# First attention: the order in which GpSimd's subtraction walks its tile

## The reference, cut to what matters

```python
disp = (x @ W_disp).reshape(B, T, nh, bd).transpose(0, 2, 1, 3)
val = (x @ W_val).reshape(B, T, nh, hs).transpose(0, 2, 1, 3)
disp_win = _windows(disp, delta)          # the last 64 positions of each t
val_win = _windows(val, delta)
strain = disp_win - disp[:, :, :, None, :]
bond_act = gelu(strain @ W_strain + rel_emb @ W_pos)
bond_logits = (bond_act @ W_bond)[..., 0]
damage_act = gelu(strain @ W_dmg + b_dmg)
damage = sigmoid((damage_act @ W_dmg_out)[..., 0] + b_dmg_out[0])
logits = bond_logits - 10.0 * damage
weights = softmax(where(cmask, logits, -inf))
out = einsum('bntd,bntde->bnte', weights, val_win) ... @ W_cproj
```

## Time and profile before

| | us |
|---|---|
| runs before, median of 3 | 2930.57 (2927.01 to 2932.88) |
| profiled execution, from its first to its last instruction | 2936.9 |
| GpSimd busy in the whole span | 1076.2 |
| of it in the changed line, 128 instructions | 531.7 |
| ScalarE, VectorE, TensorE busy in the whole span | 1983.8, 2199.1, 2435.7 |

### The profile page before, as it was taken

One profiled execution on the slowest core, in us unless ns is written; L12 is line 12 of the kernel. 1 busy time (PEld: TensorE's weight loads), 2 busy tenths in 40 slices (PEclk: granted clock), 3 DMA queues, 4 the chain that ended last, 5 costly groups with the idle time before them and its releaser, 6 DMA issues. The chain is left out here.

```text
span 2936.9 us, 34317 instructions
## 1 busy us (share of the span) xinstructions
PE 2435.7 (83%) x13037; PEld 888.8 (30%) x13037; DVE 2199.1 (75%) x3034; ACT 1983.8 (68%) x2018; POOL 1076.2 (37%) x409
## 2 busy tenths in 40 slices
PE   4678777787666766777999889998879889999996
PEld 1122222354222222444222242222544522222224
DVE  5788888867999999874889528896440467888884
ACT  5999999813733333243899758997531379999991
POOL 5999999721099999531001300013100000000000
PEclk8989999978888888888999998999989989999998
DMA  2012111110154444202212100101010121210001
GB/s 76 1 57 66 52 44 44 49 49 8 45 176 158 167 162 152 71 13 77 35 17 33 42 0 1 19 6 46 8 41 0 45 57 21 39 27 18 15 6 29
DMA packets 66671, 144.71 MB, mean 49 GB/s; under 512 B 13235, under 2 KB 29983, under 8 KB 65792
## 3 DMA queue, kind: packets, MB, share of 16 engines
q1 hardware_dynamic: 66496, 142.40, 17.0%
HBM read 117.92 MB, written 24.25 MB: 48 GB/s over the span
## 5 line engine op out<-in xcount | busy, mean ns | idle before, releaser
L828 POOL TENSOR_TENSOR l0a_diff_pool<-l0a_A,l0a_a_of_t 128x2048 f32<-128x2048 f32 x128 | 531.7, 4217 | 30.7 <-ACT l0a_a_of_t L843 30.1
L2116 ACT ACTIVATE l2x_pT<-ps 128x1024 f32<-128x1024 f32 x512 | 495.8, 1021 | 12.8 <-PE ps L2075 10.9
L2266 ACT ACTIVATE l3he_pT<-ps 128x1024 f32<-128x1024 f32 x480 | 465.0, 1021 | 32.4 <-PE ps L2201 31.0
L1438 PE MATMUL ps<-l1s_hc,all_ident 128*128 128x512 f32 x512 | 288.8, 718 | 153.0 <-POOL l1s_hc L1409 96.3
L774 DVE SCALAR_TENSOR_TENSOR l0a_diff_dve<-l0a_A,l0a_pos,ps 128x512 f32<-128x512 f32 x512 | 344.9, 742 | 30.9 <-PE ps L619 30.8
L1400 POOL TENSOR_TENSOR l1s_dBx<-l1a_dtx,l1a_Bs 128x1024 f32<-128x1024 f32 x128 | 297.4, 2353 | 111.6 <-POOLq L1134 111.6
L1424 ACT ACTIVATE ps<-l1a_dt,l1a_A 128x1024 f32<-128x1024 f32 x128 | 143.1, 1118 | 268.0 <-DVE l1s_hc L1483 215.7
L2075 PE MATMUL ps<-l2m_Qs,l2m_Ks 75*128 75x512 bf16 x1024 | 273.1, 391 | 9.8 <-PEq L2528 9.8
L2201 PE MATMUL ps<-l3h_Qs,l3h_Ks 75*128 75x512 bf16 x1024 | 266.7, 387 | 9.3 <-DVE ps L2271 9.3
L2089 PE MATMUL ps<-l2x_pT,l2m_Va 128*9 128x512 f32 x2048 | 271.6, 603 | 1.2 <-ACT l2x_pT L2116 1.2
L2670 POOL TENSOR_TENSOR l2s_E<-l2s_E,l2x_rest 128x2048 f32<-128x2048 f32 x16 | 72.7, 4544 | 514.9 <-DVEq L2393 509.8
(11 more groups left out here) (493 smaller groups left out, 3671.4 us busy)
## 6 DMA issues: line engine op xcount, KB each, us to landing
l1a_Bs<-l1a_bc SPq DMA_DIRECT2D x64, 512.0 KB, 3.6
l1s_Cs<-l1a_bc SPq DMA_DIRECT2D x64, 512.0 KB, 4.7
l0a_band_rows<-l0a_band SPq DMA_DIRECT2D x32, 512.0 KB, 5.7
l0a_band<-l0a_exps SPq DMA_DIRECT2D x14, 512.0 KB, 5.1
l2m_Ks<-l2m_parts SPq DMA_DIRECT2D x36, 128.0 KB
l2m_Qs<-l2m_parts SPq DMA_DIRECT2D x72, 64.0 KB
l3h_Qs<-l3h_parts SPq DMA_DIRECT2D x72, 64.0 KB
l0a_band<-l0a_zero SPq DMA_DIRECT2D x8, 512.0 KB, 7.4
```

What stands on the lines that cost most here:

```text
L828: pool.tensor_tensor(out, window(s), atb[:, p % 2, :].unsqueeze(1).broadcast_to([P, 4, CH]), ALU.subtract).then_inc(diff_pool, 1)
L1438: mm = pe.matmul(g.ps[:, (4 + 2 * h + q) * CH:(5 + 2 * h + q) * CH], g.ident[:, :], hc[:, m % NHC, q * CH:(q + 1) * CH], start=(n == 0), s ...
L2116: act.activation(pT[:, turn % NPT, :], g.ps[:, slot * QC:(slot + 1) * QC], ACT.Exp).then_inc(expd, 1)
L2266: act.activation(pT[:, (4 * m + j) % NPT, :], g.ps[:, slot(turn)], ACT.Exp).then_inc(expd, 1)
```

## The change

GpSimd's subtraction writes the same numbers to the same places. Output and window are handed over with their two free dimensions swapped, so that the distance (4) is the inner one and the time (512) the outer one. The subtracted row is broadcast over the inner dimension instead of the outer one.

```diff
-                    pool.tensor_tensor(out, window(s), atb[:, p % 2, :].unsqueeze(1).broadcast_to([P, 4, CH]),
-                                       ALU.subtract).then_inc(diff_pool, 1)
+                    pool.tensor_tensor(out.rearrange("p c t -> p t c"), window(s).rearrange("p c t -> p t c"),
+                                       atb[:, p % 2, :].unsqueeze(2).broadcast_to([P, CH, 4]), ALU.subtract).then_inc(diff_pool, 1)
```

## The result

The changed kernel takes 3022.74 us, median of 4 runs (3018.78 to 3029.99), against 2929.23 us for the kernel before (4 runs, 2927.01 to 2932.88): ratio 1.0322, 95% interval 1.0309 to 1.0334, so 93.5 us slower. The profiled execution has a span of 3023.1 us, 86.2 more than that of before, whose span was itself 6.3 us over its median. The forecast was 3111 us in a range of 2905 to 3270.

What follows compares the result with a forecast made beforehand. GpSimd was taken as the bound, ScalarE barely behind. 128 x 5.6 = 716.8 us replaces 535.9 (180.9 more), less 1 us behind the last subtraction: span 2936.9 to about 3117, less 6.3 gives 3111 us; range 2905 to 3270.

Steps and rivals of the forecast that it cites:

- What bounds the stage: GpSimd's 128 subtractions set the pace with 4.2 us of inner waits; ScalarE barely behind; longer subtractions paid in full.
- The direction, and that the window's step decides: Slower, chance 0.60, because GpSimd's window read enters another group of four with every element, 2048 times rather than 512.
- All four of a group alike: GpSimd's four subtractions of a group, two at 4.52 and two at 3.77 us before, should then cost the same.
- The price of a subtraction: One GpSimd subtraction goes from 4.154 to 5.6 us; 128 of them take 716.8 us, so the stage grows by 180.9.
- the likeliest case: GpSimd subtractions of 5.0 to 6.8 us, 104 to 334 us more, time 3035 to 3265 us; chance 0.53.
- the faster rival: Standing row frees GpSimd's read, 3.77 us a subtraction; ScalarE then caps the gain at 20 us: 2911 us; chance 0.30.
- the row-based 5.27: GpSimd subtraction if half of the window's moves are hidden: 3.77 + 1.5 = 5.27 us.
- The 1.46 ns: Price of one window move to its next group of four elements: 4.52 - 3.77 = 0.75 us for 512 moves.
- less the 3 us or so before the very first tile and a rest: Deduction from the 25.8 us that ScalarE waits for GpSimd, leaving 20 us to come back.
- The same: Rival: order of addresses does not matter, GpSimd's mean subtraction stays 4.1 to 4.2 us, time 2931 us; chance 0.10.
- Much slower: Rival: window read and output write both pay their jumps in full, 9.8 us a GpSimd subtraction, 3649 us; chance 0.07.

Runs made afterwards that it cites:

- the moving row: The changed kernel with the subtracted row read with step one, 512 elements four times over, instead of standing still for four: 3113.32 us, one run.
- two rows: Kernel before, each GpSimd subtraction taking whichever of two row copies, two elements apart, its window is fast against: 2924.68 us against 2931.73.
- half the work: Kernel before, but from its fifth tile on GpSimd subtracts only the first 256 of the 512 times: 2925.22 us, one run.
- The kernel with the later maxima: Version with two copies of the subtracted row, plus VectorE's four softmax-maximum steps one slot later in a phase: 2914.61 us against 2932.86.

## Why the prediction was right or wrong

*What bounds the stage*: right. GpSimd grew by 97.0 us, its inner waits fell from 4.2 to 0.8 (I had said none), and the sum of both is the loss. The work of the other engines stayed hidden. Behind GpSimd's last subtraction 1.8 us came back, where I had put 1.

*The direction, and that the window's step decides*: right, shown by the kernel with the window flat (3.85 us instead of 4.91). *All four of a group alike*: right.

*The price of a subtraction*: too high. The term was 5.6 us, 128 x 5.6 = 716.8; it measured 4.91, 628.7. That is 88 of the 88 us by which 3111 is over 3023. The forecast loss of 180 us is nearly twice the measured one, and ScalarE's waits for GpSimd rose to 110 us and not to about 200. 4.91 us lies under the own range of the likeliest case (5.0 to 6.8 us, 3035 to 3265 us); the stated range holds 3023 us only because it was stretched down to the faster rival, so that the time lies in it is luck and no merit of the price. Two things went into it wrongly. I put it a third of a microsecond over the row-based 5.27, for moves that follow too closely to hide and for the strided write; the flat write shows 0.03 us for the latter, and steps of 16 and 32 bytes in every element stay at 4.91 and 5.00. And I priced each entry of the window into another group of four as in the kernel before, with no credit for the row that stands still, which the moving row prices at 0.66 us. The 1.46 ns were no price of the window's moves alone: they hang on where the window lies relative to the row, as the shifted row shows. So the 5.27 us built on them do not follow either, however near they come. (The clock of 0.97 that the prediction names is that of 231 to 282 us in the trace; the earlier trace rows don't show it.)

*The faster rival*: its mechanism is real, the standing row does take the slow pair's extra cost away (3.85 us with the window flat), but the window's jumps cost more. Its size was wrong. I let ScalarE alone be the next bound and wrote 20 us; with two rows 7 came back, with the window flat 4 and with half the work 7, each of these two in a single run. The step that failed is "less the 3 us or so before the very first tile and a rest". The start is not 3 us but 9.6, the first four tiles, of which a faster GpSimd gave back 0.7; that leaves 17 us. The rest is 12.0 us more of waits for VectorE (12.8, of which before had 0.8), for its tile of slot 15, hidden before by ScalarE's waits for GpSimd. The kernel with the later maxima gives 18 us. That this is close to the 20 is in part luck, since the waits of ScalarE that I priced fell by only 13.7.

*The same*: wrong, since addresses alone move a subtraction from 3.77 to 5.57 us. *Much slower*: wrong, the write's jumps cost 0.03 us where this rival had them pay 3.0.

## What to carry to other kernels

On GpSimd, look at single instructions of one line before their mean: two kinds 0.75 us apart told that addresses, not work, set the time. Where two inputs both walk with step one, look at where they lie relative to each other before you change the walk: with two copies of the row, two elements apart, all four kinds of subtraction took 3.77 us. Let neither input jump by more than 8 bytes an element; a broadcast operand may stand still, and beside such reads the write may jump. Before pricing a faster engine, list for each slot who is late next, and take the filling of the pipeline out of the sum: the idle time of the waiting engine is not all given back, and once the instruction is faster, a small step moved off the late tile's path can bring as much again.

## What the runs showed of the hardware that was not expected

- GpSimd's subtraction of 128 x 2048 with both reads at step one takes 3.77 or 4.52 us by where one input lies relative to the other modulo 16 bytes, each counted from the beginning of its tile: the window two or three elements ahead is fast, none or one is slow (before, and with the row shifted by two elements, where the two kinds change places).
- With the second input standing still for four elements and the first flat, it takes 3.80 to 3.86 us wherever the first starts.
- A write in which each element lies 2048 bytes from the last costs no more than a flat one, within 0.03 us, beside a read that jumps (4.91 and 4.88 us).
- The price of a read's step is 0.17, 0.78, 1.06, 1.14 us for 8, 12, 16, 32 bytes in 2048 elements beside a standing second input.
- Standing still for four elements saves 0.66 us in 2048 beside a window that jumps by 16 bytes (5.57 to 4.91).
